# Products into an unread bank ahead of the gate rows, the first output product and the first expert block

## What is computed

```
x = x + attention(layernorm(x))      # linear attention, 8 heads, plus a 3-tap convolution
x = x + experts(layernorm(x))        # 8 experts, 2 per token, SwiGLU 256 -> 512 -> 256
x = x + rwkv_mix(layernorm(x))       # time mix (a recurrence over 512 tokens) and channel mix
x = x + experts(layernorm(x))        # same experts, same gate, again
```

## Time and profile before

| | |
|---|---|
| median of three timed runs | 1533.91 us |
| the profiled execution's own time | 1529.51 us |
| its span, first to last instruction | 1527.7 us |
| PE busy | 1332.0 us, 87% of the span |
| VectorE, ScalarE, GpSimd busy | 908.7, 670.8, 638.7 us |
| mean granted clock of TensorE over the span | 0.927 |

### The profile page before, as it was taken

How to read it: one execution, slowest core, us unless ns; L and a number is a source line. 1 busy time by engine, 2 the same in 40 slices (tenths; PEclk the granted TensorE clock), 3 DMA queues, 4 the chain that set the end, 5 groups by cost and what they waited for, 6 DMA issues and landing times. The chain is left out here.

```text
span 1527.7 us, 27930 instructions
## 1 busy us (share of the span) xinstructions
PE 1332.0 (87%) x7528; PEld 1131.5 (74%) x7529; DVE 908.7 (59%) x2122; ACT 670.8 (44%) x1506; POOL 638.7 (42%) x601
## 2 busy tenths in 40 slices
PE   4999994789999999933899999998646999999996
PEld 3989984678888888811677778777545888888885
DVE  4787875434444444438889999985163444444442
ACT  3576753223323333333776767864332323333332
POOL 3667653234455555411132222213142454555553
PEclk9899995799999999966999999999858999999998
DMA  6475761775553333360000000000027645533332
GB/s 214 170 273 193 263 241 39 248 231 125 144 126 61 57 59 55 45 203 0 1 14 29 1 28 28 28 29 29 28 97 274 181 92 135 132 56 57 54 58 36
DMA packets 100875, 157.86 MB, mean 103 GB/s; under 512 B 10256, under 2 KB 60688, under 8 KB 100816
## 3 DMA queue, kind: packets, MB, share of 16 engines
q1 hardware_dynamic: 73120, 118.67, 22.4%
q0 software_dynamic: 27264, 37.82, 15.1%
q10 hardware_dynamic: 432, 0.66, 0.2%
HBM read 95.89 MB, written 61.21 MB: 103 GB/s over the span
## 5 line engine op out<-in xcount | busy, mean ns | idle before, releaser
L1081 DVE TENSOR_TENSOR second_hT_lo<-bank,second_hT_hi 128x512 fp32r<-128x512 f32 x71 | 49.1, 692 | 170.9 <-ACT second_hT_hi L963 170.9
L1081 DVE TENSOR_TENSOR first_hT_lo<-bank,first_hT_hi 128x512 fp32r<-128x512 f32 x71 | 49.1, 692 | 165.2 <-ACT first_hT_hi L963 165.2
L929 POOL DMA_INDIRECT x_rows<-first_block_hot,first_add_token x53 | 84.0, 1586 | 127.9 <-DMA x_rows<-first_block_hot,first_add_token 62.4
L929 POOL DMA_INDIRECT out_x<-second_block_hot,second_add_token x53 | 84.0, 1586 | 124.6 <-DMA out_x<-second_block_hot,second_add_token 64.0
L155 PE MATMUL bank<-second_ring,second_xT_hi 128*128 x284 | 120.6, 425 | 9.4 <-issue 7.2
L155 PE MATMUL bank<-first_ring,first_xT_hi 128*128 x284 | 120.8, 425 | 2.2 <-DVE first_xT_lo L1069 2.1
L1771 PE MATMUL bank<-b_fv,b_hT 128*128 128x256 f32 x512 | 113.9, 381 | 0.0
L156 PE MATMUL bank<-first_ring,first_xT_hi 128*128 x284 | 113.8, 401 | 0.0
L156 PE MATMUL bank<-second_ring,second_xT_hi 128*128 x284 | 113.7, 400 | 0.0
L157 PE MATMUL bank<-first_ring,first_xT_lo 128*128 x284 | 113.6, 400 | 0.0
L157 PE MATMUL bank<-second_ring,second_xT_lo 128*128 x284 | 113.6, 400 | 0.0
(11 more groups left out here) (360 smaller groups left out, 3994.1 us busy)
## 6 DMA issues: line engine op xcount, KB each, us to landing
first_ring<-split_weights SPq DMA_DIRECT2D x96, 256.0 KB, 5.8
second_ring<-split_weights SPq DMA_DIRECT2D x96, 256.0 KB, 5.5
a_wraw<-in_L_ffn_w SPq DMA_DIRECT2D x24, 512.0 KB, 6.5
split_weights<-a_whi SPq DMA_DIRECT2D x24, 512.0 KB, 2.7
split_weights<-a_wlo SPq DMA_DIRECT2D x24, 512.0 KB, 4.0
normed_rows<-xg SPq DMA_DIRECT2D x16, 528.0 KB, 3.0
x_rows<-x SPq DMA_DIRECT2D x8, 512.0 KB, 7.0
x<-x_rows SPq DMA_DIRECT2D x8, 512.0 KB, 9.0
```

The costliest lines, as they stand in the source:

```text
L929: nc.gpsimd.indirect_dma_start(x_dram[:], bass.IndirectOffsetOnAxis(ap=add_token[q][:], axis=0), y[q], None, compute_op=ALU.add).then_inc( ...
L1081: nc.vector.tensor_tensor(hT_lo[par][:].rearrange("p k t -> p (k t)"), th_bank[par][:], hT_hi[par][:].rearrange("p k t -> p (k t)").bitcas ...
```

## The change

A helper `keep_busy` issues a given number of products, each with `start` and `stop` set, all into one bank. Nothing reads what it writes. It is called in four places in the code; the one in `phase_experts` runs in both expert phases.

```diff
+def keep_busy(nc, out, stationary, moving, times):
+    for _ in range(times):
+        nc.tensor.matmul(out, stationary, moving, start=True, stop=True)
 ...
             over_batches(pe, period)
+            keep_busy(nc, q0[:], qk_hi[:, 0, 0, :], qk_hi[:, 0, :, :].rearrange("p m n -> p (m n)"), 28)
             gate_transposes(B)
             gate_products(B)
 ...
                 last.then_inc(sent_used, 1)
+            keep_busy(nc, y_bank[:], const.ones[:], sent[0][:].rearrange("p k j b -> p (k j b)")[:, 0:H], 16)

             def transpose_x(i, q):
 ...
             pe.wait_ge(w_in, 64)
+            pe.wait_ge(kvr_evac, 6)
+            pe.wait_ge(fk_hi_ready, 1)
+            pe.wait_ge(num_ready, 1)
+            keep_busy(nc, xb_[4][:], fk_hi[:, 0, 0:P], fk_hi[:, 0, 0:N], 16)
             time_product(0)
 ...
             over_periods(pe, period)
+            pe.wait_ge(fs_ready, 2 * B)
+            keep_busy(nc, xb_[4][:], fk_hi[:, 0, 0:P], fk_hi[:, 0, 0:N], 36)
             gate_transposes(B - 1)
             gate_products(B - 1)
```

## The result

The changed kernel took 1523.34 us (median of four runs, 1521.62 to 1524.44), the kernel before on the same chip 1534.51 us (median of four, 1531.8 to 1536.41). The ratio is 0.9927, 95% interval 0.9909 to 0.9946: faster, by 8 to 14 us of 1534. The forecast of 1528.6 us was 5.3 us too high. By the time alone, the rival that every gap holds (1521.3 us) lay nearer.

What follows compares the result with a forecast made beforehand. PE was taken to bound the kernel, busy 87% of the span, with half-clock work behind idle stretches. Gates 0.6, output product 1.7 and first blocks 3.0 us sum to 5.3 us: 1533.9 - 5.3 = 1528.6 us, range 1521 to 1536 us.

Steps and rivals of the forecast that it cites:

- every gap holds: Rival, 13%: the clock stays up through the gaps at all places, gaining 12.6 us, to 1521.3 us.
- Mechanism: At four code places PE idles 7 to 26 us, then works at half clock; added dense products raise it, gaps may lower it.
- Cost of an added product: Each added product takes 0.43 us from start to start at half clock, 0.23 us at full clock.
- Gates, 0.6 us forecast: Last gates of attention and mix: clock falls before or among the transposes, gate products stay at half clock; 0.3 us each.
- Output product, 1.7 us forecast: First output product: half the time the clock holds (2.6 us), half it falls near the restart (0.9 us).
- First blocks, 3.0 us forecast: First block of both expert phases: holding 40%, worth 2.7 and 2.2 us, else 0.9 us; 1.5 us each.
- Sum: Gates, output product and first blocks together: 0.6 + 1.7 + 3.0 = 5.3 us gained.
- Starting point: The gain is taken off the median of 1533.9 us, not the profiled execution's 1529.51 us, giving 1528.6 us.
- Up too soon and down again: Rival, 24%: clock falls in the gap at nearly every place; 0 to 2.5 us gained, say 1.3 us, 1532.6 us.
- Late: Rival, 8%: added products cannot overlap their operand loads, run slower and end 11.5 us late; 1540.3 us.
- What was to show it: Gather wait ahead of block 0 about 1 us, its `up` 2.8 or 3.5 to 4.5, output 3.5 to 5.2, gate products 3.58.

Runs made afterwards that it cites:

- e2: Kernel before plus only the sixteen products ahead of the first expert block, in both expert phases; ratio 0.9965 to the kernel before, 1526.15 us.
- e7: Changed kernel with the sixteen 512-column products in the expert phases replaced by thirty of 72 columns; ratio 0.9965 to the kernel before, 1524.85 us.
- e12: Changed kernel with eight products in place of sixteen in the expert phases; ratio 0.9975 to the kernel before, 1526.0 us.
- e5: The changed kernel again, unedited, for a second trace and timing; ratio 0.9943 to the kernel before, 1519.82 us.
- e6: Changed kernel with 41 and 50 products ahead of the last gates in place of 28 and 36; ratio 0.9938 to the kernel before, 1520.21 us.
- e8: e6 plus 22 products ahead of the first low key product in the first mix period; ratio 0.9910 to the kernel before, 1515.14 us.
- e4: Kernel before plus only the 28 and 36 products ahead of the two last gates; ratio 0.9987 to the kernel before, 1528.16 us.
- e10: e8 with sixteen products ahead of the 64 routing products, 28 behind them, four behind block 0's transposes; ratio 0.9928 to the kernel before, 1520.65 us.
- e11: Changed kernel with 32 products in place of sixteen in the expert phases; ratio 0.9976 to the kernel before, 1527.21 us.

## Why the prediction was right, step by step

- **Mechanism.** Right: dense products raise the clock (e2, e7, e12), and whether it outlives the idle time behind them decides the rest (e5, e6, e12). That the gain adds up over the places agrees with e2 to e5 but is no sharper than their intervals.
- **Cost of an added product.** Right. 0.43 us and 0.23 us were taken; the sixteen took 5.1 to 6.4 us in the ten places of the expert phases, with a rise after 2.6 us (e5) to 5.4 us (e8). Forecast were 5.9 us with a rise after 5. (The end of those ahead of the output product, put at 712.7 to 714.1 us, is 713.0 to 713.9 us by the same prices; nothing hangs on it.)
- **Gates, 0.6 us forecast.** The reading was right: the clock falls near the restart and the gate products stay at 3.58 us, in eleven of twelve places (the twelfth is e4's mix gate, behind a short gap). The term was mis-sized by half: 25.68 - 25.08 = 0.60 and 26.84 - 26.26 = 0.58, so 1.2 us. The clock outlives the gap of 3.35 us, so that most of the 0.93 us on the transposes is won; the forecast let it fall before or among them and took 0.3 us.
- **Output product, 1.7 us forecast.** Measured 2.3 us. The clock held as in the upper bound, and the bound itself was 2.3 us beside the mean of four kernels without (13.74), not the 2.6 us of one profile. I took holding at even odds; it held in ten of ten, behind gaps of 1.04 to 2.59 us. The gap of 1.97 us that spoke against it was weighed too high. In e6, e12 and e5 gaps of 2.65, 2.20 and 1.67 us ahead of a first block were followed by a fall, where two short transposes and another idle 1.07 us stand behind the gap and not sixteen dense products. That the surroundings make the difference is likely and was not tested by itself.
- **First blocks, 3.0 us forecast.** Measured 2 x (6.57 - 4.94) = 3.3 us, with holding in seven of ten places where I gave 40%. Holding is worth less than I took, 6.57 - 4.42 = 2.15 us each and not 2.7 and 2.2: the profile before had the longest first block of eight (7.04 us).
- **Sum.** 5.3 us forecast, 1.2 + 2.3 + 3.3 = 6.8 us by places. Timed, it was 8.7 us (5.4 to 11.9 by the interval of e5), and 11.2 us (8.3 to 14.0) beside a median of four. By e5 the missing 1.9 us are inside the interval. One candidate: the rest of the first expert phase, behind the first block, took 360.6 us in the mean of four kernels without added products there and 359.0 us in five with sixteen; but 362.0 in e10 and e11, and the second phase shows no such difference (362.3 each). e7 and e12, whose first blocks ran at half clock, took 359.1 and 359.4 us there, so it is not the first block's clock that makes it. It stays open.
- **Starting point.** I took the gain off 1533.9 us, a median of three. With 19 to 35 runs the median before was 1530.2 to 1530.5 us. From there the same forecast would give 1525.1 us, and the changed kernel took 1519.8 us. The first measured time was inside the range of 1521 to 1536 us with a gain twice the forecast; the mechanism was not luck, but the place sum is 1.5 us over the forecast, and the other 4.4 us of the first 11.2 us are not explained by any place. The base of 1534.5 us, 4 us over the later medians, is a likely part of them.
- **Rivals.** *Every gap holds*: refuted at the gates (e4's first, e5), true at the output product, true in seven of ten at the first blocks. *Up too soon and down again*: true at the gates and in e2's second phase, e5's and e6's first. *Late*: refuted, an idle rest of 0.10 to 2.65 us was left ahead of block 0 in nine of ten places (none in e8's second phase); e11 fits its way of pricing: 5.1 us of lateness over the two phases came with 5.1 us in the time. The Trainium skill ("TensorE: Matmul & The Clock Gate", section "Why this matters for your kernels") advises against gaps over about 3 us. The gates' 3.35 to 3.50 us and the output product's 2.31 us agree; the first block of e5, 1.67 us, a short transpose and 1.07 us, does not, nor does that of e2, 0.87 us with the same behind it.
- **What was to show it.** The gather wait ahead of block 0 shrank from 7.25 to 0.35 us (first forecast 1 us), `up` of block 0 took 2.90 us, the output product 3.56 us, gate products 3.58 us. That the two first profiles agree here does not make them typical, as e5's 5.93 us shows. The two numbers that would have proved it wrong did not come: gate products of 1.95 us, and `L1133` (L1124 before) later after its gather.

## What to carry to other kernels

Where PE idles for several us and then has short work for which another engine waits, unread products of 512 columns with ready operands turn the idle time into clock, if they end shortly ahead of the data. Behind ends up to 0.6 us early the clock held through all or nearly all of the work at every place here; at the first blocks it was a draw from 0.87 us on. Late products delay everything (e11), and an end 3 us early gave nothing at the first block (e12) and 0.6 us of 2.56 at a gate. Count them by the clock with which the stretch starts, 0.43 us each until the clock is up, and leave room: fifty products took 11.62 us in one kernel and 13.20 us in another. Judge such a change place by place over several profiles: 2 us per place was not told by twelve runs.

## What was not expected of the hardware

- Busy time does not raise the clock by itself: 94 products of 72 columns, 21.00 us busy of 21.10, at 1.2 GHz (e7); and in e10, where the clock was up as such products began, it was down 1.8 us later and stayed down for the 12.56 us that they were busy. The sixteen gate products of 8 columns in e6, 1.95 and 2.00 us of them, ran at 2.4 GHz.
- The fall comes late: behind gaps of 3.35 us (first profile), 1.67 us (e5) and 0.87 us (e2) PE had already resumed at 2.4 GHz. The clock fell up to 2.6 us later, in e5 and e2 among dense products, in the first profile in the idle stretch behind the transposes. The gap ahead of the output product (1.04 to 2.59 us) was followed by no fall in any of ten kernels.
- The rise behind the start of dense products took from 2.6 us (e5) to 5.1 us (e11) for the same products at the same place of the first expert phase. Ahead of the output product it took over 6 us in e11: from 708.87 to 714.90 us PE was busy throughout at 0.50.
